# A transformer tower on one core: ScalarE makes the rounded high part of the normalised rows, GpSimd only the low part, and GpSimd's order of normalising changes

## The chip, the cores and the metric

The kernel runs on one core of one Trainium2 chip. The metric is the device time of one execution in microseconds (us). Engines are named as in the profile: PE is TensorE, ACT is ScalarE, DVE is VectorE, POOL is GpSimd, SP is SyncE, which only issues transfers here. Each engine works through its own instructions strictly in order and waits on semaphores for the others.

## The reference

32 sequences of 512 tokens with 64 features pass through an embedding and four layers. Each layer normalises its input row by row (no learned scale) and adds its result back to it:

```
h = tok(x)                                # token row plus position row
h = h + attn0(layernorm(h))               # softmax(q k^T / 8) x,  q = x Wq^T, k = x Wk^T
h = h + ffn0(layernorm(h))                # relu(Wi x), two layers routed to one of 16 experts, Wo
h = h + attn1(layernorm(h))               # the same with biases, values and an output projection
h = h + ffn1(layernorm(h))                # 8 experts of 64 -> 128 -> 64 with gelu, top 2 kept
```

The layer norm is `(x - mean) / sqrt(var + 1e-5)` over the 64 features.

## The kernel before, in words

All rows stay in SBUF in `H` (128 partitions, 32 sequences, 4 tiles of 128 tokens, 64 features). The kernel is written out engine by engine. After the embedding come four stages, called a0, f0, a1 and f1 (attention 0, routed layer, attention 1, mixture). In each, every engine runs a body once for each of the 32 sequences; a body i does the main work of sequence i and looks ahead. All that crosses engines is a count on a semaphore.

**The norm of a sequence** runs two to five sequences ahead of the stage that uses it:

- DVE sums the rows (`norm_sum`, L645).
- POOL centres them (`norm_centre`): a mean of 128x4 (L363), then `XC` = row minus mean (L369).
- DVE squares `XC`, sums and makes the variance (`norm_squares`: L649, L651, L653) and raises `var_ready`.
- POOL scales (`norm_scale`): a power of -0.5 on 128x4 (L375), `XN` = `XC` times it in full fp32 (L382), the same product once more into the rounded type fp32r, the high part in the left half of `XS` (L387), and the low part, `XN` minus the high part, in the right half (L390), which raises `xs_ready`.
- PE transposes `XS` (`turn`, L928), ACT copies the result into `X2` (`evac_x`, L463), and the stage's matmuls use it.

`XC`, `XS` and `X2` have two buffers, `XN` has four, since the attention reads it as its values. So in the attention stages the write of `XN` for sequence i+3 waits for the count `o_ps` that PE raises with the last matmul of `values` for sequence i-1 (L1013).

**Where the bodies stand.** POOL's body i does `norm_centre` of i+4 and then `norm_scale` of i+3. DVE's attention body i begins with `norm_squares` of i+4 and goes on with `norm_sum` of i+5, the low part of the queries (L729), `finish` of i-1 (L742, L744, L746) and the four row maxima of i+1 (L735). PE's attention body computes `spread_max` (L992), `project` of i+1 (L968, L969), the turn of i+2, the scores (L1004, L1005) with `turn_back` (L953) between them, and then, in this order, two `scores_for_max` of i+1 (L979), half of `values` of i, two more `scores_for_max`, which need the first two maxima, and the other half of `values`. ACT's attention body takes out the values (L485), the maxima (L504) and the queries (L491), makes the four exponentials (L511) and ends with `evac_x` of i+2.

In f0, PE's body i starts with the turn of i+2 (L928) and ends with the first routed layer of sequence i (L1087, the second four of eight matmuls). ACT's body takes out `X2` (L463) and the input layer (L521), then the values of an earlier sequence (L483), and ends with the two relus of L534, which wait for exactly that routed layer.

Of the kernel before, what the change touches and what calls it, by code (L numbers as in the profile page):

```python
# [22 lines left out]
ALU = mybir.AluOpType  # L23
ACT = mybir.ActivationFunctionType
# [3 lines left out]
NSEQ, SEQ, D = 32, 512, 64  # L28
# [13 lines left out]
CONSTS = 7  # L42
# [100 lines left out]
def sweep(eng, body, start=0, first=4, last=NSEQ - 6):  # L143


    for i in range(start, first):
        body(i, i % 2)
    with eng.Fori(first // 2, last // 2) as pair:
        body(pair * 2, 0)
        body(pair * 2 + 1, 1)  # L150
    for i in range(last, NSEQ):
        body(i, i % 2)
# [14 lines left out]
def known(i):  # L167
    return isinstance(i, int)


def has(i):

    return not known(i) or i < NSEQ


def tower_kernel(nc, tokens, route, pack, experts, out, ids_dram, pos_dram):
# [3 lines left out]
    with ExitStack() as ctx:  # L180
# [165 lines left out]
        @block.gpsimd  # L346
        def _(pool):
            pl = nc.gpsimd

            pl.memset(half[:, :], -0.5).then_inc(consts_set, 1)  # L350
            pl.memset(ninv[:, :], -1.0 / D).then_inc(consts_set, 1)
            pl.memset(MK[:, :, :], 0.0).then_inc(consts_set, 1)
            pl.memset(XN[:, :, :, 0:1], 1.0).then_inc(consts_set, 1)
            pl.memset(f32(XS[:, :, :, 0:1]), 1.0).then_inc(consts_set, 1)
            pl.memset(f32(XS[:, :, :, D:D + 1]), 0.0).then_inc(consts_set, 1)
            pl.memset(R1[:, :], 0.0).then_inc(consts_set, 1)

            pool.wait_ge(consts_set, CONSTS)

            def norm_centre(s, before, phase, i, par):  # L360

                pool.wait_ge(s.sum_ready, i + 1)
                pl.tensor_tensor(stat[:, par, 1, :], stat[:, par, 0, :], ninv[:, :], ALU.mult).then_inc(mean_done, 1)  # L363
                pool.wait_ge(mean_done, phase * NSEQ + i + 1)
                if not known(i) or i >= 2:
                    pool.wait_ge(s.var_ready, i - 1)
                elif before is not None:
                    pool.wait_ge(before.var_ready, NSEQ - 1 + i)
                pl.tensor_tensor(XC[:, par, :, :], hb(i), over(stat[:, par, 1, :], D), ALU.add)\  # L369
                    .then_inc(s.xc_ready, 1)  # L370

            def norm_scale(s, before, phase, i, par, lane):

                pool.wait_ge(s.var_ready, i + 1)
                pl.tensor_tensor(stat[:, par, 3, :], stat[:, par, 2, :], half[:, :], ALU.pow).then_inc(sigma_done, 1)  # L375
                pool.wait_ge(sigma_done, phase * NSEQ + i + 1)
                if (s is a0 or s is a1) and (not known(i) or i >= 4):
                    pool.wait_ge(s.o_ps, i - 3)
                elif (before is a0 or before is a1) and known(i) and i < 4:
                    pool.wait_ge(before.o_ps, NSEQ - 3 + i)  # L380
                scale = over(stat[:, par, 3, :], D - 1)
                pl.tensor_tensor(XN[:, lane, :, 1:D], XC[:, par, :, 1:D], scale, ALU.mult).then_inc(xn_done, 1)  # L382
                if not known(i) or i >= 2:
                    pool.wait_ge(s.xt_ready, i - 1)
                elif before is not None:
                    pool.wait_ge(before.xt_ready, NSEQ - 1 + i)
                pl.tensor_tensor(XS[:, par, :, 1:D], XC[:, par, :, 1:D], scale, ALU.mult).then_inc(s.xh_done, 1)  # L387
                pool.wait_ge(xn_done, phase * NSEQ + i + 1)
                pool.wait_ge(s.xh_done, i + 1)
                pl.tensor_tensor(XS[:, par, :, D + 1:2 * D], XN[:, lane, :, 1:D], f32(XS[:, par, :, 1:D]),  # L390
                                 ALU.subtract).then_inc(s.xs_ready, 1)

            def centre_on(s, before, after, phase, i, par):

                if has(i):
                    norm_centre(s, before, phase, i, par)
                elif after is not None:
                    norm_centre(after, s, phase + 1, i - NSEQ, par)

            def scale_on(s, before, after, phase, i, par, lane):  # L400
                if has(i):
                    norm_scale(s, before, phase, i, par, lane)
                elif after is not None:
                    norm_scale(after, s, phase + 1, i - NSEQ, par, lane)

            def norms(s, before, after, phase):
                def body(i, par, lane):
                    centre_on(s, before, after, phase, i + 4, par)
                    scale_on(s, before, after, phase, i + 3, 1 - par, (lane + 3) % 4)

                sweep4(pool, body)


            norm_centre(a0, None, 0, 0, 0)
            for i in range(3):
                norm_centre(a0, None, 0, i + 1, 1 - i % 2)
                norm_scale(a0, None, 0, i, i % 2, i)
            norms(a0, None, f0, 0)
            norms(f0, a0, a1, 1)
            norms(a1, f0, f1, 2)  # L420

            norms(f1, a1, None, 3)
# [3 lines left out]
        def _(act):  # L426
# [21 lines left out]
            for i in range(EARLY + HIGHS, EARLY + HIGHS + 2):  # L448
# [2 lines left out]
                           w("ident")[D:P, D:D + NEXP1].unsqueeze(2).to_broadcast([P - D, NEXP1, HID]),  # L451
                           ACT.Copy, scale=-OFF).then_inc(high_set, 1)
            sweep(act, embed, start=EARLY + HIGHS + 2, first=EARLY + HIGHS + 2)

            def evac_x(s, i, par):
                act.wait_ge(s.xt_ready, i + 1)
# [31 lines left out]
            def attention(s, before, after, layer, meanwhile):  # L488
                def evac_q(i, par):
                    act.wait_ge(s.q_ps, i + 1)  # L490
                    sc_.activation(QH[:, par, :], bank[1][:, :], ACT.Copy).then_inc(s.qh_ready, 1)  # L491

                if before is None:
                    evac_x(s, 0, 0)
                evac_q(0, 0)
                if before is None:
                    evac_x(s, 1, 1)

                def body(i, par):
                    if not known(i) or i >= 1:  # L500
                        evac_o(s, before, bank[6], i - 1, 1 - par)
                    act.wait_ge(s.m_ps, i + 1)
                    act.wait_ge(s.ql_ready, i + 1)
                    sc_.activation(Q2[0:1, par, :], bank[7][0:1, :], ACT.Copy).then_inc(s.m_ready, 1)  # L504
                    if has(i + 1):
                        evac_q(i + 1, 1 - par)
                    for kt in range(NT):
                        act.wait_ge(s.st_ps, i * NT + (kt + 1))
                        if kt == 0 and (not known(i) or i >= 2):
                            act.wait_ge(s.o_ps, i - 1)  # L510
                        sc_.activation(PT[:, par, kt, :], bank[4 + kt % 2][:, :], ACT.Exp,  # L511
                                       scale=SCALE).then_inc(s.e_ready, 1)
                    evac_x_on(s, after, i + 2, par)

                sweep(act, body)
                meanwhile()
                evac_o(s, before, bank[6], NSEQ - 1, 1)

# [3 lines left out]

            attention(a0, None, f0, 0, lambda: ffn0_in(0, 0))

            def ffn0(i, par):
                evac_x_on(f0, a1, i + 2, par)
                if has(i + 1):
                    ffn0_in(i + 1, 1 - par)
                if not known(i) or i >= 2:
                    evac_o(f0, a0, bank[4], i - 2, par)  # L530
                act.wait_ge(f0.l0_ps, i + 1)
                act.wait_ge(f0.wc_ready, i + 1)
                for g in range(NG):
                    ins = sc_.activation(group(F1[:, par, :], g), group(bank[2][:, :], g), ACT.Relu,  # L534
                                         bias=WC[:, par, g, HID:HID + 1])
                ins.then_inc(f0.h1_ready, 1)

            def group(ap, g):

                return ap.rearrange("k (t g p) -> k g t p", t=NT, g=NG)[:, g, :, :]  # L540

            sweep(act, ffn0)
            evac_o(f0, a0, bank[4], NSEQ - 2, 0)
            evac_o(f0, a0, bank[4], NSEQ - 1, 1)
            attention(a1, f0, f1, 1, lambda: None)
# [13 lines left out]
                    act.wait_ge(f1.down_ps, i * NEXP1 + (e - 7))  # L559
                sc_.activation(G[:, e, :], bank[3 + e % 2][:, :], ACT.Gelu).then_inc(f1.gelu_ready, 1)  # L560

            def ffn1(i, par):
                for e in range(4):
                    gelu(i, e)
                if not known(i) or i >= 1:
                    evac_o(f1, a1, bank[6 - par], i - 1, 1 - par)
                gelu(i, 4)
                gelu(i, 5)
                if has(i + 1):
                    masks(i + 1, 1 - par)  # L570
                gelu(i, 6)
                gelu(i, 7)
                if has(i + 2):
                    evac_x(f1, i + 2, par)

            sweep(act, ffn1)
            evac_o(f1, a1, bank[6], NSEQ - 1, 1)


# [725 lines left out]
```

## Time and profile before

| what | value |
|---|---|
| median of 3 runs | 1053.97 us (1051.72 to 1054.2) |
| the profiled execution: its own time | 1054.74 us |
| its span, first to last instruction | 1052.9 us |
| busy: PE, DVE, ACT, POOL | 956.7, 660.6, 547.1, 491.1 us |
| mean granted clock of TensorE | 0.98 |
| embedding and start | about 0 to 84 us |
| a0 / f0 / a1 / f1 | to about 319 / 461 / 706 / 1053 us |

The first column of a timeline row is the start, the second the duration. The stage limits are read off the first and last starts of each stage's matmuls, to a few microseconds.

### The profile page before, as it was taken

The page shows a single profiled execution, that of the slowest core. Times are in us where ns is not written, and L with a number is a line of the kernel's source. Part 1 is how long each engine was busy: PE and PEld are TensorE (multiplying, and loading weights), DVE is VectorE, ACT ScalarE, POOL GpSimd, SP SyncE. Part 2 cuts the span into 40 slices and gives each one's busy share as a digit, 9 for nine tenths or more (in the row PEclk, how much of TensorE's full clock was granted, in tenths as well). Part 3 has the DMA queues.
Part 4 walks back from the last instruction along what each step waited for, and adds up shares of the span by engine and source line. Part 5 has one row for each costly group of instructions (what it writes and reads, how often), then busy time and mean ns, then how long its engine had stood idle before and what let it go on. Part 6 is the DMA issues. An engine that isn't in the chain of part 4 may idle for free.

```text
span 1052.9 us, 20503 instructions
## 1 busy us (share of the span) xinstructions
PE 956.7 (91%) x5964; PEld 612.7 (58%) x5964; DVE 660.6 (63%) x1864; ACT 547.1 (52%) x1065; POOL 491.1 (47%) x779
## 2 busy tenths in 40 slices
PE   0479999999998888879999999999999999999998
PEld 0456666666665555556666666665555555555554
DVE  1586888887887888877888878873333434343311
ACT  0234555555555555535555555565555555555554
POOL 0026454554547888974545455453333333333310
PEclk9868999999999999999999999999999999999999
DMA  8930000000001212200000000000000000000000
GB/s 8 254 108 1 2 0 0 0 0 0 1 1 49 58 55 60 61 21 2 1 0 0 0 0 1 1 1 7 16 11 15 10 12 13 10 15 10 16 11 21
DMA packets 31309, 22.35 MB, mean 21 GB/s; under 512 B 14498, under 2 KB 26914, under 8 KB 31266
## 3 DMA queue, kind: packets, MB, share of 16 engines
q1 hardware_dynamic: 31266, 21.81, 9.5%
q8 instruction: 23, 0.38, 0.2%
q14 instruction: 20, 0.16, 0.1%
HBM read 17.54 MB, written 4.26 MB: 21 GB/s over the span
## 4 chain that ended last, share of the span: by engine, by line
PE 70%; DVE 10%; POOL 7%; issue 5%; DMA 4%; ACT 2%; DVEq 0%; SPq 0%; POOLq 0%
PE bank L1178 12%; PE bank L1158 7%; PE bank L1004 6%; PE bank L1013 6%; DVE nmax L735 6%; PE bank L1005 6%; PE bank L979 5%; PE bank L1159 5%; PE bank L928 5%; PE bank L992 4%; PE bank L953 3%; POOL stat L375 2%; DMA pos<-posn 2%; PE bank L1135 2%; PE bank L1168 2%
## 5 line engine op out<-in xcount | busy, mean ns | idle before, releaser
L560 ACT ACTIVATE PT<-bank 128x512 f32<-128x512 f32 x256 | 142.2, 595 | 99.9 <-PE bank L1159 99.1
L735 DVE TENSOR_REDUCE nmax<-bank 128x1 fp32r<-128x512 f32 x256 | 164.9, 686 | 34.0 <-PE bank L979 29.5
L382 POOL TENSOR_TENSOR XN<-XC,stat 128x252 f32<-128x252 f32 x128 | 85.3, 667 | 214.0 <-PE bank L1013 209.0
L511 ACT ACTIVATE PT<-bank 128x512 f32<-128x512 f32 x256 | 139.1, 595 | 46.1 <-PE bank L1005 46.1
L375 POOL TENSOR_TENSOR stat<-stat,half 128x4 f32<-128x4 f32 x128 | 134.3, 1049 | 38.0 <-DVE stat L653 35.4
L795 DVE TENSOR_TENSOR H<-H,bank 128x256 f32 (+1 forms) x64 | 26.9, 421 | 186.8 <-PE bank L958 186.8
L1013 PE MATMUL bank<-PT,XN 128*64 128x256 f32 x1024 | 138.3, 392 | 0.0
L1178 PE MATMUL bank<-PT,W 128*64 128x256 f32 x1024 | 137.2, 388 | 0.0
L387 POOL TENSOR_TENSOR XS<-XC,stat 128x252 fp32r<-128x252 f32 x128 | 77.3, 604 | 103.6 <-PE bank L928 103.6
L1158 PE MATMUL bank<-X,WH 128*128 128x512 f32 x256 | 116.0, 453 | 1.0 <-ACT K L551 0.8
L1004 PE MATMUL bank<-QH,X 128*128 128x512 f32 x256 | 115.8, 452 | 0.6 <-ACT Q L504 0.4
L485 ACT ACTIVATE OT<-bank 128x256 f32<-128x256 f32 x96 | 37.1, 386 | 133.8 <-PE bank L1013 132.0
L390 POOL TENSOR_TENSOR XS<-XN,XS 128x252 fp32r<-128x252 f32 x128 | 94.5, 738 | 18.7 <-POOL XS L387 0.5
L463 ACT ACTIVATE X<-bank 128x512 fp32r<-128x512 f32 x128 | 76.5, 597 | 51.2 <-PE bank L928 51.2
L1005 PE MATMUL bank<-Q,X 128*128 128x512 f32 x256 | 101.6, 397 | 0.0
L1159 PE MATMUL bank<-K,WL 80*128 80x512 f32 x256 | 100.8, 394 | 0.0
L928 PE MATMUL bank<-W,XS 128*128 128x128 f32 x512 | 80.3, 280 | 21.8 <-POOL XS L390 21.1
L1178 PEld LDWEIGHTS bank<-PT,W 128*64 128x64 f32 x1024 | 64.8, 136 | 57.9 <-issue 34.6
L1013 PEld LDWEIGHTS bank<-PT,XN 128*64 128x64 f32 x1024 | 62.2, 136 | 58.1 <-ACT PT L511 22.7
L979 PE MATMUL bank<-X,QH 128*128 128x512 f32 x256 | 88.3, 426 | 1.7 <-DVE nmax L735 1.4
L369 POOL TENSOR_TENSOR XC<-H,stat 128x256 f32<-128x256 f32 x128 | 79.1, 618 | 20.0 <-POOL stat L363 16.3
L363 POOL TENSOR_TENSOR stat<-stat,ninv 128x4 f32<-128x4 f32 x128 | 30.7, 240 | 122.7 <-DVE stat L645 122.7
(124 smaller groups left out, 1620.1 us busy)
## 6 DMA issues: line engine op xcount, KB each, us to landing
WR<-experts SPq DMA_DIRECT2D x64, 129.0 KB, 2.1
PT<-ids SPq DMA_DIRECT2D x16, 256.0 KB, 5.3
out<-H SPq DMA_DIRECT2D x32, 128.0 KB, 1.7
posb<-pos SPq DMA_DIRECT2D x16, 192.0 KB, 5.7
W<-pack SPq DMA_DIRECT2D x5, 263.0 KB, 6.4
W<-pack SPq DMA_DIRECT2D x1, 262.5 KB, 9.7
W<-pack SPq DMA_DIRECT2D x1, 65.0 KB, 4.7
tk<-tokens SPq DMA_DIRECT2D x1, 64.0 KB, 4.5
```

The source lines that it names most:

```text
L375: pl.tensor_tensor(stat[:, par, 3, :], stat[:, par, 2, :], half[:, :], ALU.pow).then_inc(sigma_done, 1)
L511: sc_.activation(PT[:, par, kt, :], bank[4 + kt % 2][:, :], ACT.Exp, scale=SCALE).then_inc(s.e_ready, 1)
L560: sc_.activation(G[:, e, :], bank[3 + e % 2][:, :], ACT.Gelu).then_inc(f1.gelu_ready, 1)
L735: v.tensor_reduce(nmax[:, par, t:t + 1], bank[2 + t % 2][:, :], axis=AX, op=ALU.max, negate=True).then_inc(s.max_ready, 1)
L928: last = nc.tensor.transpose(bank[0][:, t * P:(t + 1) * P], f32(XS[:, par, t, :]), w("ident"))
L979: mm(bank[2 + t % 2][:, :], QH[:, par, t * P:(t + 1) * P], X2[:, par, :], start=True, stop=True).then_inc(s.s_ps, 1)
L1004: mm(o, X2[:, par, cols], QH[:, par, :], start=True, stop=False)
L1005: mm(o, X2[:, par, cols], Q2[:, par, :], start=False, stop=True).then_inc(s.st_ps, 1)
L1013: last = mm(bank[6][h * D:(h + 1) * D, 0:HALF], XN[:, lane, kt, :], PT[:, par, kt, h * HALF:(h + 1) * HALF], start=(kt == 0), stop=(kt == ...
L1158: mm(o, WH[:, a:a + HID], X2[:, par, :], start=True, stop=False)
L1159: mm(o, WL[0:D + 2 * NEXP1, a:a + HID], K2[0:D + 2 * NEXP1, par, :], start=False, stop=True)\
L1178: last = mm(bank[5 + par][h * D:(h + 1) * D, 0:HALF], w2[:, e, :], G[:, e, h * HALF:(h + 1) * HALF], start=False, stop=(e == NEXP1 - 1))
```

## The change

Three things change. ScalarE copies `XN` into the high part (`high`, an activation with the function Copy), where GpSimd multiplied a second time; GpSimd keeps only the subtraction (`norm_low`). GpSimd's body i is now power and `XN` of i+3, then centring of i+4, then the low part of i+3. The copy of sequence i+3 is the last instruction in each of ScalarE's bodies i, and at the start ScalarE makes the copies of sequences 0, 1 and 2 before its first `evac_x`. The programs of PE and DVE are the same instructions in the same order.

```diff
--- before.py
+++ after.py
@@ -380,12 +380,9 @@
                     pool.wait_ge(before.o_ps, NSEQ - 3 + i)
                 scale = over(stat[:, par, 3, :], D - 1)
                 pl.tensor_tensor(XN[:, lane, :, 1:D], XC[:, par, :, 1:D], scale, ALU.mult).then_inc(xn_done, 1)
-                if not known(i) or i >= 2:
-                    pool.wait_ge(s.xt_ready, i - 1)
-                elif before is not None:
-                    pool.wait_ge(before.xt_ready, NSEQ - 1 + i)
-                pl.tensor_tensor(XS[:, par, :, 1:D], XC[:, par, :, 1:D], scale, ALU.mult).then_inc(s.xh_done, 1)
-                pool.wait_ge(xn_done, phase * NSEQ + i + 1)
+
+            def norm_low(s, i, par, lane):
+
                 pool.wait_ge(s.xh_done, i + 1)
                 pl.tensor_tensor(XS[:, par, :, D + 1:2 * D], XN[:, lane, :, 1:D], f32(XS[:, par, :, 1:D]),
                                  ALU.subtract).then_inc(s.xs_ready, 1)
@@ -403,10 +400,17 @@
                 elif after is not None:
                     norm_scale(after, s, phase + 1, i - NSEQ, par, lane)
 
+            def low_on(s, after, i, par, lane):
+                if has(i):
+                    norm_low(s, i, par, lane)
+                elif after is not None:
+                    norm_low(after, i - NSEQ, par, lane)
+
             def norms(s, before, after, phase):
                 def body(i, par, lane):
+                    scale_on(s, before, after, phase, i + 3, 1 - par, (lane + 3) % 4)
                     centre_on(s, before, after, phase, i + 4, par)
-                    scale_on(s, before, after, phase, i + 3, 1 - par, (lane + 3) % 4)
+                    low_on(s, after, i + 3, 1 - par, (lane + 3) % 4)
 
                 sweep4(pool, body)
 
@@ -415,6 +419,7 @@
             for i in range(3):
                 norm_centre(a0, None, 0, i + 1, 1 - i % 2)
                 norm_scale(a0, None, 0, i, i % 2, i)
+                norm_low(a0, i, i % 2, i)
             norms(a0, None, f0, 0)
             norms(f0, a0, a1, 1)
             norms(a1, f0, f1, 2)
```

The same for ScalarE:

```diff
@@ -451,6 +456,26 @@
                            w("ident")[D:P, D:D + NEXP1].unsqueeze(2).to_broadcast([P - D, NEXP1, HID]),
                            ACT.Copy, scale=-OFF).then_inc(high_set, 1)
             sweep(act, embed, start=EARLY + HIGHS + 2, first=EARLY + HIGHS + 2)
+
+            def high(s, before, phase, i, par, lane):
+
+                act.wait_ge(xn_done, phase * NSEQ + i + 1)
+                if not known(i) or i >= 2:
+                    act.wait_ge(s.xt_ready, i - 1)
+                elif before is not None:
+                    act.wait_ge(before.xt_ready, NSEQ - 1 + i)
+                act.wait_ge(consts_set, CONSTS)
+                sc_.activation(XS[:, par, :, 1:D], XN[:, lane, :, 1:D], ACT.Copy).then_inc(s.xh_done, 1)
+
+            def high_on(s, before, after, phase, i, par, lane):
+
+                if has(i):
+                    high(s, before, phase, i, par, lane)
+                elif after is not None:
+                    high(after, s, phase + 1, i - NSEQ, par, lane)
+
+            for i in range(3):
+                high(a0, None, 0, i, i % 2, i)
 
             def evac_x(s, i, par):
                 act.wait_ge(s.xt_ready, i + 1)
@@ -496,7 +521,7 @@
                 if before is None:
                     evac_x(s, 1, 1)
 
-                def body(i, par):
+                def body(i, par, lane):
                     if not known(i) or i >= 1:
                         evac_o(s, before, bank[6], i - 1, 1 - par)
                     act.wait_ge(s.m_ps, i + 1)
@@ -511,8 +536,9 @@
                         sc_.activation(PT[:, par, kt, :], bank[4 + kt % 2][:, :], ACT.Exp,
                                        scale=SCALE).then_inc(s.e_ready, 1)
                     evac_x_on(s, after, i + 2, par)
-
-                sweep(act, body)
+                    high_on(s, before, after, layer * 2, i + 3, 1 - par, (lane + 3) % 4)
+
+                sweep4(act, body)
                 meanwhile()
                 evac_o(s, before, bank[6], NSEQ - 1, 1)
 
@@ -522,7 +548,7 @@
 
             attention(a0, None, f0, 0, lambda: ffn0_in(0, 0))
 
-            def ffn0(i, par):
+            def ffn0(i, par, lane):
                 evac_x_on(f0, a1, i + 2, par)
                 if has(i + 1):
                     ffn0_in(i + 1, 1 - par)
@@ -534,12 +560,13 @@
                     ins = sc_.activation(group(F1[:, par, :], g), group(bank[2][:, :], g), ACT.Relu,
                                          bias=WC[:, par, g, HID:HID + 1])
                 ins.then_inc(f0.h1_ready, 1)
+                high_on(f0, a0, a1, 1, i + 3, 1 - par, (lane + 3) % 4)
 
             def group(ap, g):
 
                 return ap.rearrange("k (t g p) -> k g t p", t=NT, g=NG)[:, g, :, :]
 
-            sweep(act, ffn0)
+            sweep4(act, ffn0)
             evac_o(f0, a0, bank[4], NSEQ - 2, 0)
             evac_o(f0, a0, bank[4], NSEQ - 1, 1)
             attention(a1, f0, f1, 1, lambda: None)
@@ -559,7 +586,7 @@
                     act.wait_ge(f1.down_ps, i * NEXP1 + (e - 7))
                 sc_.activation(G[:, e, :], bank[3 + e % 2][:, :], ACT.Gelu).then_inc(f1.gelu_ready, 1)
 
-            def ffn1(i, par):
+            def ffn1(i, par, lane):
                 for e in range(4):
                     gelu(i, e)
                 if not known(i) or i >= 1:
@@ -572,8 +599,9 @@
                 gelu(i, 7)
                 if has(i + 2):
                     evac_x(f1, i + 2, par)
-
-            sweep(act, ffn1)
+                high_on(f1, a1, None, 3, i + 3, 1 - par, (lane + 3) % 4)
+
+            sweep4(act, ffn1)
             evac_o(f1, a1, bank[6], NSEQ - 1, 1)
```

**GpSimd in an attention stage.** The rows are one body of the program of before, with the first row of the next; L382 is the product that makes `XN`.

```order
L363 TENSOR_TENSOR stat<-stat,ninv 128x4 [waits a0_sum_ready]
L369 TENSOR_TENSOR XC<-H,stat 128x256 [waits a0_var_ready,mean_done]
L375 TENSOR_TENSOR stat<-stat,half 128x4 [waits a0_var_ready]
L382 TENSOR_TENSOR XN<-XC,stat 128x4x63 [waits a0_o_ps,sigma_done]
L387 TENSOR_TENSOR XS<-XC,stat 128x4x63 [waits a0_xt_ready]
L390 TENSOR_TENSOR XS<-XN,XS 128x4x63 [waits a0_xh_done,xn_done]
L363 TENSOR_TENSOR stat<-stat,ninv 128x4 [waits a0_sum_ready]
```

And of the changed program, where the subtraction has line 387:

```order
L375 TENSOR_TENSOR stat<-stat,half 128x4 [waits a0_var_ready]
L382 TENSOR_TENSOR XN<-XC,stat 128x4x63 [waits a0_o_ps,sigma_done]
L363 TENSOR_TENSOR stat<-stat,ninv 128x4 [waits a0_sum_ready]
L369 TENSOR_TENSOR XC<-H,stat 128x256 [waits a0_var_ready,mean_done]
L387 TENSOR_TENSOR XS<-XN,XS 128x4x63 [waits a0_xh_done]
L375 TENSOR_TENSOR stat<-stat,half 128x4 [waits a0_var_ready]
```

The centring (L363, L369) stood ahead of the instruction that waits for `o_ps` and now stands behind it.

**ScalarE in f0.** One body of before, and the first row of the next:

```order
L463 ACTIVATE X<-bank 128x512 [waits f0_xt_ready]
L521 ACTIVATE F<-bank 128x512 [waits f0_wi_ps]
L483 ACTIVATE OT<-bank,W 128x256 [waits f0_back_ps,f0_o_ps]
L534 ACTIVATE F<-bank,WC 128x4x64 [waits f0_wc_ready,f0_l0_ps]
L534 ACTIVATE F<-bank,WC 128x4x64
L463 ACTIVATE X<-bank 128x512 [waits f0_xt_ready]
```

The same place in the changed program:

```order
L488 ACTIVATE X<-bank 128x512 [waits f0_xt_ready]
L547 ACTIVATE F<-bank 128x512 [waits f0_wi_ps]
L508 ACTIVATE OT<-bank,W 128x256 [waits f0_back_ps,f0_o_ps]
L560 ACTIVATE F<-bank,WC 128x4x64 [waits f0_wc_ready,f0_l0_ps]
L560 ACTIVATE F<-bank,WC 128x4x64
L462 REGISTER_ALU
L468 ACTIVATE XS<-XN 128x4x63 [waits consts_set,f0_xt_ready,xn_done]
```

The copy stands behind the relus, which wait for `l0_ps`, the count of the routed layer with which PE ends its body.

**ScalarE at the start**, in the changed program; H is the end of the embedding, X the first `evac_x`:

```order
L436 ACTIVATE H<-bank 128x256 [waits emb_ready] x6
L468 ACTIVATE XS<-XN 128x4x63 [waits consts_set,xn_done] x2
L468 ACTIVATE XS<-XN 128x4x63 [waits consts_set,a0_xt_ready,xn_done]
L488 ACTIVATE X<-bank 128x512 [waits a0_xt_ready]
L516 ACTIVATE QH<-bank 128x512 [waits a0_q_ps]
```

Before, X followed H directly; the three copies of L468 now stand between them.

## Rows read from the trace of the kernel before

**Rows 1.** Windows of a0 and f0: us; busy PE, PEld, DVE, ACT, POOL; clock.

```profile
113.00:282.00 169.00, 165.43 (x968) 110.30 (x968) 136.79 (x277) 95.75 (x185) 87.30 (x139) 1.00 0.00 0
...
319.00:461.00 142.00, 120.38 (x640) 79.79 (x640) 118.86 (x282) 75.87 (x159) 124.69 (x188) 1.00 0.21 56
```

**Rows 2.** The chain that ended last, in f0: start us, us, what.

```profile
338.22 1.13 POOL stat L375
...
410.54 1.13 POOL stat L375
```

**Rows 3.** Timeline of f0: start us, us, then idle time before in brackets.

```profile
390.41 0.72 POOL L390 TENSOR_TENSOR XS<-XN,XS 128x252 fp32r<-128x252 f32 x1
...
391.18 0.66 PE L928 MATMUL bank<-W,XS 128*128 128x128 f32 x4 [0.66 <-POOL XS L390]
...
393.10 1.89 PE L1087 MATMUL bank<-F,WC 128*128 128x256 f32 x8
...
395.03 0.84 ACT L534 ACTIVATE F<-bank,WC 128x256 f32<-128x256 f32 x2 [1.54 <-PE bank L1087]
```

**Rows 4.** Timeline of a0, one body.

```profile
197.52 0.41 DVE L649 TENSOR_TENSOR SQ<-XC 128x256 f32<-128x256 f32 x1
...
197.68 0.72 POOL L382 TENSOR_TENSOR XN<-XC,stat 128x252 f32<-128x252 f32 x1 [3.26 <-PE bank L1013]
...
198.91 0.41 DVE L645 TENSOR_REDUCE stat<-H 128x4 f32 x1
...
200.27 0.61 POOL L369 TENSOR_TENSOR XC<-H,stat 128x256 f32<-128x256 f32 x1 [0.27 <-POOL stat L363]
...
200.68 0.18 DVE L742 RECIPROCAL rec<-bank 128x4 f32<-128x4 f32 x1 [0.49 <-PE bank L953]
...
201.92 1.29 DVE L735 TENSOR_REDUCE nmax<-bank 128x1 fp32r<-128x512 f32 x2
...
202.18 0.60 ACT L463 ACTIVATE X<-bank 128x512 fp32r<-128x512 f32 x1
...
203.70 1.08 PE L1013 MATMUL bank<-PT,XN 128*64 128x256 f32 x8
...
204.94 0.73 POOL L382 TENSOR_TENSOR XN<-XC,stat 128x252 f32<-128x252 f32 x1 [3.08 <-PE bank L1013]
```

**Rows 5.** Timeline of the start of a0.

```profile
77.95 0.38 ACT L431 ACTIVATE H<-bank 128x256 f32<-128x256 f32 x1 [2.62 <-PE bank L904]
...
78.61 0.61 POOL L382 TENSOR_TENSOR XN<-XC,stat 128x252 f32<-128x252 f32 x1
...
79.17 0.60 POOL L387 TENSOR_TENSOR XS<-XC,stat 128x252 fp32r<-128x252 f32 x1
...
79.71 0.60 ACT L463 ACTIVATE X<-bank 128x512 fp32r<-128x512 f32 x1 [1.38 <-PE bank L928]
...
79.92 0.72 POOL L390 TENSOR_TENSOR XS<-XN,XS 128x252 fp32r<-128x252 f32 x1
...
80.60 0.20 POOL L363 TENSOR_TENSOR stat<-stat,ninv 128x4 f32<-128x4 f32 x1
...
80.88 0.61 POOL L369 TENSOR_TENSOR XC<-H,stat 128x256 f32<-128x256 f32 x1
...
81.45 1.02 POOL L375 TENSOR_TENSOR stat<-stat,half 128x4 f32<-128x4 f32 x1
...
81.53 0.42 DVE L649 TENSOR_TENSOR SQ<-XC 128x256 f32<-128x256 f32 x1 [2.54 <-POOL XC L369]
...
82.52 0.69 DVE L729 TENSOR_TENSOR Q<-bank,QH 128x512 fp32r<-128x512 f32 x1
...
82.55 0.61 POOL L382 TENSOR_TENSOR XN<-XC,stat 128x252 f32<-128x252 f32 x1
```

**Rows 6.** Groups by form, f0 from 360 to 396: busy us, mean ns.

```profile
L649 DVE TENSOR_TENSOR SQ<-XC 128x256 f32<-128x256 f32 x8 | 6.0, 755 | 0.0
```

**Rows 7.** Timeline of f1.

```profile
783.36 0.60 ACT L560 ACTIVATE PT<-bank 128x512 f32<-128x512 f32 x1 [0.80 <-PE bank L1159]
```

## The prediction
> **What bounds the kernel now.** I read the page first: PE is busy for 91% of the span, POOL for 47%, so a relief of POOL can pay only where POOL is what PE waits for. The windows view shows where that is [rows 1]: in a0 PE is busy for 165.4 of 169 us and POOL for 87.3; in f0 it is the other way round, 120.4 of 142 us against POOL's 124.7. The chain that ended last then says what sets f0's pace: it goes through POOL's power (L375) again and again, and from 338.22 to 410.54 us lie 16 bodies, so a body of f0 takes 72.32 / 16 = 4.52 us [rows 2]. The timeline shows the wait itself: PE sat idle for 0.66 us until POOL's low part (L390), 390.41 + 0.72 = 391.13, let it turn at 391.18 [rows 3]. PE's own body runs from there to the end of the last routed matmul, 393.10 + 1.89 = 394.99, that is 3.81 us. In the attention the pace is 204.94 - 197.68 = 7.26 us a body in the piece shown [rows 4], and two things are to be seen there. POOL's product `XN` starts only 0.16 us after PE's last `values` matmul (203.70 + 1.08 = 204.78), after 3.08 us of idle time. And DVE has no long wait: squares, sum, low part of the queries, reciprocal at 200.68, then maxima at 201.92, on the third of which PE's next scores depend.
>
> **The change in f0: a new loop through three engines.** One multiplication of about 0.60 us (the form of 79.17 in [rows 5]) leaves POOL's body. But the copy that replaces it stands at the end of ScalarE's body, behind the relus, and these wait for the end of PE's body. POOL's low part waits for the copy, and PE's next body begins with the turn that waits for the low part. So all of it comes after one another, once per body:
>
> - turn to relus: 391.18 to 395.03, 3.85 us [rows 3]
> - the two relus: 0.84 us [rows 3]
> - the copy of 128x252: no copy of this form is in the trace. ScalarE's 128x256 copy out of PSUM took 0.38 us, the 128x512 one 0.60 us [rows 5]; these are the bounds, and I take 0.40, by the nearer form
> - from ScalarE to POOL: no row; POOL follows PE by 0.16 us [rows 4], DVE follows POOL by 0.04 us (81.53 after 80.88 + 0.61, [rows 5]). I take 0.08
> - the low part 0.72 us, and 0.05 us to PE's turn [rows 3]
>
> The sum is 5.94 us a body instead of 4.52. Sequence i+3 of ScalarE's body i is what PE's body i+1 turns, so every one of the 31 steps from a body of f0 to the next has it: 31 x 1.42 = 44 us more. Bounds: with 0.38 and 0.04 it is 5.88 us (42 us), with 0.60 and 0.16 it is 6.22 us (53 us). The relief of POOL is worth nothing there, since POOL then waits for the copy.
>
> **The change in the attention stages: the centring comes behind the wait.** POOL's centring of i+4 was done before POOL waited for the values of i-1; DVE's squares at the head of its body found it finished (200.27 + 0.61 = 200.88, squares at 204.79 or so). Now POOL does it behind `XN`, which can't start before those values are done. DVE's squares wait for it, and behind them on DVE stand the sum, the low part of the queries, `finish` and the maxima; PE's third and fourth `scores_for_max` wait for the first two maxima, and the second half of the values stands behind these on PE. That closes a loop from `XN` to the next `XN`:
>
> - `XN` to the mean 0.56 (78.61 to 79.17, the spacing of two such products), mean to `XC` 0.28, `XC` 0.61, to the squares 0.04 us [rows 5]
> - squares to the next instruction of DVE 0.99 us (81.53 to 82.52), the sum 0.41 [rows 4], the low part of the queries 0.69 us [rows 5]
> - reciprocal to maxima 1.24, two maxima 1.29, from their end (203.21) to the second half of the values 0.49, these 1.08, to `XN` 0.16 us [rows 4]
>
> Sum: 7.84 us, against 7.26 in the same piece. I take 0.60 us a body. This loop exists in bodies 1 to 30 of each attention, 60 times: 36 us. Its upper bound takes the slower durations of the same instructions, where POOL and DVE worked at once: 0.72 for `XN`, 0.47 from mean to `XC`, 1.39 from squares to sum [rows 4], which makes 8.59 us, and 80 us in all. The lower bound is 0.3 us a body, 18 us, if DVE's instructions overlap a little more than these spacings.
>
> A rule bears on the choice between 0.99 and 1.39. In f0, the squares took 0.755 us in the mean [rows 6], with POOL at work, and 0.41 us in a0 [rows 4]. The Trainium skill, SBUF — State Buffer, section "Who interferes with whom", says that a VectorE instruction with two SBUF inputs and a GpSimd instruction that reads SBUF lock each other out, while a reduction never contends. By that rule the squares of the new loop run alone, for POOL has nothing to do then but wait for the copy; by it the sum stays at 7.84 us, by the contended rows at 8.59.
>
> **What else of it is hidden in the attention.** The copy itself: ScalarE's `evac_x` ends at 202.18 + 0.60 = 202.78, the next thing it waits for comes at 204.8 [rows 4]; there is room for 0.40 us. Behind it POOL has the low part and the power: 202.78 + 0.40 + 0.08 + 0.68 (79.92 to 80.60) + 1.10 (81.45 to 82.55) = 205.04 us [rows 4, 5], and in the longer body `XN` can start at 197.68 + 7.84 = 205.52. That cover is only 0.5 us; if it is gone, each us beyond it costs 60 us.
>
> **f1.** ScalarE has 0.80 us of idle time between its first and second gelu [rows 7], after the place where the copy comes in, so its 0.40 us cost nothing; POOL's whole body has over 10 us there. Nothing is late next: the turn of that sequence comes a full body later. I count 0.
>
> **The start.** ScalarE's first `evac_x` was at 79.71 us [rows 5]. Now it comes behind three copies, and the third needs `XN` of sequence 2, for which POOL must first have finished two low parts, each behind a copy. Step by step from the end of the embedding at 77.95 + 0.38 = 78.33: copy to 78.73; low part (0.08 + 0.68) 79.49; centring of 2 (0.28 + 0.57) 80.34; power 1.10 and `XN` 0.61, 82.05; copy 0.48, 82.53; low part 83.29; centring of 3, 84.14; power and `XN` 85.85; copy 86.33. The first `evac_x` is 6.6 us late, and PE's first projection stands behind it, so all of the rest. Bounds 5 and 9 us.
>
> **The sum** is made against the profiled execution's own 1054.74 us (span 1052.9), 0.8 us over the median of the runs: 1054.7 + 6.6 + 44 + 36 + 0 = 1141 us. I forecast 1141 us, 8% slower.
>
> **The rivals.**
>
> - *Only f0 and the start cost* (chance 0.08): DVE makes up for the late squares. For it: DVE waits 0.49 us for PE before the reciprocal [rows 4], which is slack. Against: that slack is used up in the sum above. 1054.7 + 6.6 + 44 = 1105 us.
> - *The attention loop is contended or the 0.5 us of cover is gone* (0.12): 8.59 us a body, 1054.7 + 6.6 + 44 + 80 = 1185 us. For it: POOL and DVE do slow each other in [rows 6]. Against: POOL is idle while this loop is on DVE.
> - *The relief of POOL decides* (0.03), the other side: if the copy came to POOL in time in f0, POOL's body would be 0.60 us shorter, 3.92 us, just above PE's 3.81. 31 x 0.60 = 19 us off, 1036 us, provided that the attention hides its part too. It decides from the point at which the copy is done before POOL gets to the low part, which the place behind the relus excludes by about 3 us.
> - *The losses and the relief cancel, or nothing changes* (0.02): about 1054 us.
>
> The forecast, that all three parts cost about what is worked out, has 0.75.
>
> **How the numbers follow.** The likeliest case has its own range of 1120 to 1170 us (lower: 5 + 42 + 18; upper: 9 + 53 + 53, that is nearly 0.9 us an attention body). The range for 8 in 10 reaches towards both slower rivals, 1108 to 1180 us. A measurement of this kernel tells about 0.3% from no change. Faster by more than that has only the relief, 0.03; within it 0.02; slower 0.95.
>
> **What would show it.** In the changed profile: in f0, PE's turn waits about 2.1 us a body for POOL's low part, POOL's low part for ScalarE's copy, and a body takes 5.9 us; ScalarE's copies of `XN` take 0.40 us, 128 of them. In the attention, DVE's squares wait for `XC` in each body, for roughly 2 us, and a body takes 7.8 us or a little more; the centring starts about 0.6 us after `XN`. The first `evac_x` is near 86 us. f1 is as long as before. The prediction is wrong if the copy in f0 is found done when POOL comes to the low part, or if DVE's squares do not wait in the attention.

## The result, and the profile after

The changed kernel takes 1151.99 us in the median of 4 runs (1148.59 to 1153.64), the kernel before 1054.09 us in its 4 runs beside it: a ratio of 1.0927, with a 95% interval of 1.0895 to 1.0959. The forecast was 1141 us.

The page of the changed kernel: span and busy times, then the granted clock in the 40 slices.

```profile
span 1150.1 us, 20414 instructions
...
PE 1001.0 (87%) x5964; PEld 628.2 (55%) x5964; DVE 627.8 (55%) x1864; ACT 587.4 (51%) x1193; POOL 406.2 (35%) x651
...
PEclk9768999999998888888999999999999999999999
```

PE has the same 5964 matmuls as before and 44 us more of busy time, POOL 85 us less. In slices 13 to 19, which are f0, the clock is at 8 tenths; before, it stood at 9 in f0. The windows view cuts out a0 and f0, beside [rows 1] (the same columns).

```profile
112.00:332.00 220.00, 213.16 (x1209) 137.56 (x1211) 155.08 (x347) 127.99 (x259) 88.78 (x145) 1.00 0.00 0
345.00:540.00 195.00, 134.00 (x571) 84.71 (x572) 106.70 (x251) 78.86 (x171) 97.13 (x145) 0.85 0.14 38
```

In f0 PE is busy for 134 of 195 us, and the granted clock is 0.85. To compare stages I take ScalarE's `evac_o` of sequence 0 in each attention, and the last, which every kernel has:

| stretch | before, us | after, us | more |
|---|---|---|---|
| to the first `evac_o` of a0 | 94.83 | 98.54 | 3.7 |
| a0, to its last | 226.2 | 235.2 | 9.0 |
| f0, to the first of a1 | 158.1 | 231.8 | 73.7 |
| a1, to its last | 226.1 | 234.4 | 8.4 |
| f1 and the end of the span | 347.7 | 350.1 | 2.4 |

The sum is the 97.2 us between the two spans. The first row also holds the embedding, whose end moves by some us from trace to trace: in f0_early, fill8, fill4 and fill2, which have the changed kernel's program up to there, the first `evac_o` starts at 97.92, 97.68, 99.84 and 101.23 us. Who waits is in the waits view of the changed kernel: us in total, times, longest.

```profile
POOL XS L387 <- ACT XS L468: 580.8, 128, 12.8
...
DVE SQ L677 <- POOL XC L369: 132.4, 70, 3.3
...
PE bank L956 <- POOL XS L387: 68.8, 32, 2.2
...
POOL XN L382 <- PE bank L1041: 37.1, 60, 1.0
```

POOL's low part waits for ScalarE's copy in all 128 bodies, PE's turn for the low part in the 32 of f0, and DVE's squares for the centring, 132 us in all; before, the turn waited 21 us in all, the first wait was not there, and the squares waited 3.2 us in all. They can be seen one by one. First a body of f0 in the timeline:

```profile
420.20 0.41 ACT L468 ACTIVATE XS<-XN 128x252 fp32r<-128x252 f32 x1
...
420.69 0.84 POOL L387 TENSOR_TENSOR XS<-XN,XS 128x252 fp32r<-128x252 f32 x1 [3.78 <-ACT XS L468]
...
421.59 0.66 PE L956 MATMUL bank<-W,XS 128*128 128x128 f32 x4 [2.15 <-POOL XS L387]
...
425.43 0.84 ACT L560 ACTIVATE F<-bank,WC 128x256 f32<-128x256 f32 x2 [1.54 <-PE bank L1115]
...
426.16 0.41 ACT L468 ACTIVATE XS<-XN 128x252 fp32r<-128x252 f32 x1
...
426.65 0.84 POOL L387 TENSOR_TENSOR XS<-XN,XS 128x252 fp32r<-128x252 f32 x1 [2.31 <-ACT XS L468]
...
427.54 0.79 PE L956 MATMUL bank<-W,XS 128*128 128x128 f32 x4 [2.15 <-POOL XS L387]
```

The turn at 421.59, the relus at 425.43, the copy at 426.16, the low part at 426.65 and the next turn at 427.54: 5.95 us, each behind the other, in place of the pace of [rows 2]. The turn follows at once where [rows 3] had it wait 0.66 us; here it waits 2.15. But the next body is longer. The windows view, cut at four turns in a row:

```profile
421.59:427.54 5.95, 3.80 (x20) 2.50 (x21) 3.83 (x10) 2.70 (x6) 3.38 (x6) 1.00 0.17 44
427.54:435.04 7.50, 5.35 (x20) 3.32 (x21) 3.84 (x10) 2.81 (x6) 3.38 (x6) 0.77 0.13 35
435.04:441.00 5.96, 3.82 (x21) 2.50 (x21) 3.84 (x10) 2.68 (x6) 3.38 (x6) 1.00 0.17 44
441.00:448.51 7.51, 5.36 (x21) 3.26 (x21) 3.84 (x10) 2.81 (x6) 3.39 (x6) 0.77 0.12 35
```

The same 20 or 21 matmuls take 3.80 us in one body and 5.35 in the next, at a clock of 0.77, a mixture of the levels 2.4 and 1.2 GHz; the 1.55 us are the whole difference between 5.95 and 7.50 us. Over 29 bodies, from the turn at 345.50 to that at 544.30 us, the mean is 6.86 us: 12 of them take 5.95 to 6.05 us and 17 take 7.36 to 7.52.

The attention, one body of a0 in the timeline, beside [rows 4]:

```profile
213.75 0.61 POOL L382 TENSOR_TENSOR XN<-XC,stat 128x252 f32<-128x252 f32 x1 [0.82 <-PE bank L1041]
...
214.77 0.61 POOL L369 TENSOR_TENSOR XC<-H,stat 128x256 f32<-128x256 f32 x1 [0.26 <-POOL stat L363]
...
215.42 0.43 DVE L677 TENSOR_TENSOR SQ<-XC 128x256 f32<-128x256 f32 x1 [2.19 <-POOL XC L369]
...
216.46 0.42 DVE L673 TENSOR_REDUCE stat<-H 128x4 f32 x1
...
217.39 0.17 DVE L770 RECIPROCAL rec<-bank 128x4 f32<-128x4 f32 x1
...
218.09 0.59 ACT L488 ACTIVATE X<-bank 128x512 fp32r<-128x512 f32 x1
...
218.51 2.57 DVE L763 TENSOR_REDUCE nmax<-bank 128x1 fp32r<-128x512 f32 x4
218.57 0.42 ACT L468 ACTIVATE XS<-XN 128x252 fp32r<-128x252 f32 x1
219.07 0.72 POOL L387 TENSOR_TENSOR XS<-XN,XS 128x252 fp32r<-128x252 f32 x1 [3.68 <-ACT XS L468]
...
220.27 1.08 PE L1041 MATMUL bank<-PT,XN 128*64 128x256 f32 x8
...
221.45 0.61 POOL L382 TENSOR_TENSOR XN<-XC,stat 128x252 f32<-128x252 f32 x1 [0.68 <-PE bank L1041]
```

The squares waited 2.19 us for the centring that ended at 214.77 + 0.61 = 215.38, and from `XN` to `XN` it is 7.70 us. The four maxima now follow one another without a gap, 2.57 us; before, they came in pairs with PE between them.

### The profile page after: what moved, and what is told of

Read it like the earlier page. It is cut to its first block, busy times and chain, and to the rows that moved or that the text cites. A ratio compares the mean times of both kernels' runs of the same rounds, so it can differ in the third digit from the quotient of the medians.

```text
span 1150.1 us, 20414 instructions
## 1 busy us (share of the span) xinstructions
PE 1001.0 (87%) x5964; PEld 628.2 (55%) x5964; DVE 627.8 (55%) x1864; ACT 587.4 (51%) x1193; POOL 406.2 (35%) x651
## 4 chain that ended last, share of the span: by engine, by line
PE 53%; DVE 17%; issue 10%; POOL 10%; ACT 5%; DMA 4%; DVEq 1%; POOLq 0%; SPq 0%; ACTq 0%
PE bank L1206 11%; PE bank L1186 6%; DVE nmax L763 6%; PE bank L1041 5%; PE bank L1187 5%; PE bank L1115 4%; PE bank L956 4%; POOL XC L369 3%; POOL XS L387 3%; DVE Q L757 3%; PE bank L1007 3%; ACT X L488 2%; PE bank L986 2%; DVE SQ L677 2%; PE bank L1124 2%
## 5 line engine op out<-in xcount | busy, mean ns | idle before, releaser
L956 PE MATMUL bank<-W,XS 128*128 128x128 f32 x512 | 84.4, 290 | 68.8 <-POOL XS L387 68.8
L375 POOL TENSOR_TENSOR stat<-stat,half 128x4 f32<-128x4 f32 x128 | 137.0, 1071 | 0.3 <-DVE stat L681 0.3
L677 DVE TENSOR_TENSOR SQ<-XC 128x256 f32<-128x256 f32 x128 | 54.0, 422 | 132.4 <-POOL XC L369 132.4
L1007 PE MATMUL bank<-X,QH 128*128 128x512 f32 x256 | 104.2, 451 | 14.3 <-DVE nmax L763 4.8
L956 PEld LDWEIGHTS bank<-W,XS 128*128 128x128 f32 x512 | 63.9, 147 | 90.4 <-POOL XS L387 56.1
L382 POOL TENSOR_TENSOR XN<-XC,stat 128x252 f32<-128x252 f32 x128 | 77.8, 608 | 42.5 <-PE bank L1041 37.1
L369 POOL TENSOR_TENSOR XC<-H,stat 128x256 f32<-128x256 f32 x128 | 78.9, 617 | 19.7 <-POOL stat L363 16.0
```

Source lines behind the costliest of these rows:

```text
L956: last = nc.tensor.transpose(bank[0][:, t * P:(t + 1) * P], f32(XS[:, par, t, :]), w("ident"))
L1007: mm(bank[2 + t % 2][:, :], QH[:, par, t * P:(t + 1) * P], X2[:, par, :], start=True, stop=True).then_inc(s.s_ps, 1)
```

## The experiments

Each is one edit, on the changed kernel unless it says otherwise.

**f0_early: the copy in f0 ahead of the relus.**

```diff
             def ffn0(i, par, lane):
...
+                high_on(f0, a0, a1, 1, i + 3, 1 - par, (lane + 3) % 4)
                 act.wait_ge(f0.l0_ps, i + 1)
...
-                high_on(f0, a0, a1, 1, i + 3, 1 - par, (lane + 3) % 4)
```

> The changed kernel, but in f0 ScalarE's copy stands ahead of the relus instead of behind them. Theory A (in f0 the copy behind the relus makes one loop turn - routed layer - relus - copy - low part - turn): the loop opens; the next limit is the variance, through power, product, centring and low part over two bodies, (4.9 + 3.6) / 2 = 4.3 us a body instead of the 6.85 us in the mean of the changed kernel, and with PE's idle time the lower clock in f0 goes too. 31 x 2.5 = 77 us less: about 1075 us. Rival B (the bodies of 7.5 us in f0 come from something else, such as the loads of experts): every second body stays long, and no more than 31 x 1.4 = 44 us go: about 1108 us.

Measured: 1080.96 us, a ratio of 1.0270 (1.0234 to 1.0306) to the kernel before, 71 us less than the changed kernel. A body of f0 takes 4.60 us (22 bodies between 346.65 and 447.97 us), and the windows view of this kernel gives f0 its clock back:

```profile
345.00:450.00 105.00, 87.51 (x460) 57.43 (x460) 88.49 (x207) 63.54 (x136) 75.80 (x115) 1.00 0.22 57
```

No body is long any more, so rival B is out. The body is 4.60 and not 4.3 us. As the timeline reads, and no run tests it, this is because the squares run beside POOL's low part and take 0.92 us there, which is then on the path that leads through the variance; POOL's power waits 1.01 us for it:

```profile
422.45 0.72 POOL L387 TENSOR_TENSOR XS<-XN,XS 128x252 fp32r<-128x252 f32 x1
...
422.53 0.92 DVE L677 TENSOR_TENSOR SQ<-XC 128x256 f32<-128x256 f32 x1
...
423.94 0.17 DVE L681 TENSOR_SCALAR stat<-var 128x4 f32<-128x4 f32 x1
...
424.18 1.27 POOL L375 TENSOR_TENSOR stat<-stat,half 128x4 f32<-128x4 f32 x1 [1.01 <-DVE stat L681]
```

**centre_first: GpSimd centres first again.**

```diff
                 def body(i, par, lane):
-                    scale_on(s, before, after, phase, i + 3, 1 - par, (lane + 3) % 4)
                     centre_on(s, before, after, phase, i + 4, par)
+                    scale_on(s, before, after, phase, i + 3, 1 - par, (lane + 3) % 4)
                     low_on(s, after, i + 3, 1 - par, (lane + 3) % 4)
```

> The changed kernel with one thing back: GpSimd centres before power and product, as before; the copy stays on ScalarE where it is. Theory A (the attention lost its time by the centring behind the wait for the values): both attentions go back to about 7.3 us a body, the squares hardly wait; f0 keeps its loop and its clock. About 35 us less than the changed kernel: 1117 us. Rival C (ScalarE's extra 0.4 us a body, or the low part that comes late behind it, costs the time): the attention stays at 7.8 us a body, no difference.

Measured: 1134.64 us, a ratio of 1.0766 (1.0740 to 1.0792), 17 us less than the changed kernel. Both attentions are back at 7.31 us a body (30 bodies between 101.75 and 320.89 us), and f0 is as bad as in the changed kernel, at a clock of 0.86. Rival C is out: ScalarE has its 0.41 us in every body here and it costs nothing. With the copy on ScalarE, the order costs 17 us in all, not 35, for the attention of the changed kernel took 7.63 us a body in the mean, not 7.9. The groups view from 120 to 300 us shows the squares without their wait:

```profile
L677 DVE TENSOR_TENSOR SQ<-XC 128x256 f32<-128x256 f32 x25 | 10.6, 423 | 1.1 <-POOL XC L369 1.1
```

**order_only: the kernel before, with GpSimd's order alone.**

```diff
                 def body(i, par, lane):
-                    centre_on(s, before, after, phase, i + 4, par)
                     scale_on(s, before, after, phase, i + 3, 1 - par, (lane + 3) % 4)
+                    centre_on(s, before, after, phase, i + 4, par)
+                    low_on(s, before, after, phase, i + 3, 1 - par, (lane + 3) % 4)
```

with `norm_low` holding GpSimd's second product and the subtraction.

> The kernel before with GpSimd's order alone changed: power and product, then centring, then high part (still GpSimd's multiplication) and low part. ScalarE as before. Theory A: the attention has the new loop without any copy, 7.8 us a body, 60 x 0.5 = 30 us more; f0 is limited by the variance through power, product, centring and both halves, (4.9 + 4.2) / 2 = 4.6 us a body, 3 us more: about 1088 us, and PE keeps its clock. Rival C: without the copy on ScalarE the attention stays at 7.3 us, about 1057 us.

Measured: 1109.41 us, a ratio of 1.0524 (1.0497 to 1.0551), so 55 us more than the kernel before without any copy on ScalarE. The attention takes 8.01 us a body (30 bodies, 94.15 to 334.57 us), 0.7 us more than before; f0 4.9 us at a clock of 1.00. 60 x 0.69 and 31 x 0.4 us make 54 us. In f0 0.1 us a body was expected; the squares run beside POOL there and take 0.85 us in the mean. Rival C is out here too. That it is slower in the attention than the changed kernel was not expected. Its squares, in the same view and stretch, and those of the changed kernel:

```profile
L660 DVE TENSOR_TENSOR SQ<-XC 128x256 f32<-128x256 f32 x23 | 18.7, 811 | 46.7 <-POOL XC L369 46.7
```

```profile
L677 DVE TENSOR_TENSOR SQ<-XC 128x256 f32<-128x256 f32 x24 | 10.2, 426 | 48.9 <-POOL XC L369 48.9
```

0.81 against 0.43 us, which is the whole 0.38 us between 8.01 and 7.63: here POOL has its second product to do just when the squares have become free to run, in the changed kernel it waits for the copy. Both wait about 2 us for the centring.

**fill8, fill4 and fill2: work that nobody reads.** PE gets 8, 4 or 2 matmuls more at the end of each body of f0.

```diff
                 routed(i, par, 0)
+                for _ in range(8):          # 4, 2
+                    mm(bank[5][:, 0:HALF], w("ident"), W[:, 0:HALF], start=True, stop=True)
```

> The changed kernel with extra work: in f0, PE ends each body with 8 matmuls of 128x256 whose result nobody reads, in a bank that f0 does not use. They take about 1.9 us of the 2.15 us that PE waits for the low part. Theory D (the bodies of 7.5 us are bodies at the lower granted clock, which came with PE's idle time): the granted clock in f0 stays at 1.00, all bodies take about 6.0 us, and the kernel gets faster by doing more, 31 x 0.9 = 27 us less: about 1125 us. Rival B (something else makes every second body long): no gain, or up to 31 us slower where the extra matmuls come on top.

Measured: 1160.59 us, a ratio of 1.1016 (1.0988 to 1.1044), 9 us slower than the changed kernel. The price of the matmuls was mis-sized: each stands as two in the profile, and the 8 take 3.62 us, not 1.9:

```profile
404.86 3.62 PE L1146 MATMUL bank<-W 128*128 128x256 f32 x16
...
408.31 0.60 PE L956 MATMUL bank<-W,XS 128*128 128x128 f32 x4
```

But no body is long or short any more (6.96 to 7.12 us), and the clock is 1.00. So the clock half of the theory held and the time was inconclusive; hence the two smaller ones.

> The changed kernel with 4 idle matmuls at the end of PE's body in f0. The 8 of the run before took 3.6 us a body, more than the 2.15 us of waiting, and f0 ran at 7.04 us a body at a granted clock of 1.00. Theory D (the long bodies of the changed kernel are bodies at the lower clock): 4 take 1.8 us and fit into the wait, every body takes 5.96 us, clock 1.00, 31 x 0.9 = 27 us less than the changed kernel: about 1124 us. Rival B (the wait for the low part is what it is, and the clock follows something else): no gain, 1152 us.

Measured: 1128.16 us, a ratio of 1.0674 (1.0648 to 1.0701).

> The same with 2 idle matmuls, 0.9 us of the 2.15 us. Theory D: part of the long bodies go, 5.96 to 6.85 us a body, 1124 to 1152 us. Rival B: 1152 us.

Measured: 1127.18 us, a ratio of 1.0667 (1.0640 to 1.0695). Both are 24 to 25 us faster than the changed kernel, by doing more, and in both a body of f0 takes 5.96 us in the mean, with none over 6.05. The stretch of f0 in the table above, 231.8 us in the changed kernel, is 206.8 us in fill4 and 205.6 in fill2. The windows view of fill2 in f0:

```profile
345.00:510.00 165.00, 128.70 (x664) 89.80 (x664) 105.23 (x248) 74.52 (x167) 94.30 (x140) 1.00 0.17 44
```

With theory D two matmuls were expected to give back a part and gave back all. Rival B is out: the loop through the low part still sets the 5.96 us, and the long bodies were the lower clock.

**start_only: another order at ScalarE's start.**

```diff
-            for i in range(3):
-                high(a0, None, 0, i, i % 2, i)
...
                 if before is None:
+                    high(s, None, 0, 0, 0, 0)
                     evac_x(s, 0, 0)
+                    high(s, None, 0, 1, 1, 1)
                 evac_q(0, 0)
                 if before is None:
                     evac_x(s, 1, 1)
+                    high(s, None, 0, 2, 0, 2)
```

> The changed kernel with ScalarE's first instructions in another order: copy 0, first evac_x, copy 1, first queries, second evac_x, copy 2. Theory A: the first evac_x comes 1.4 us after the embedding's end and the low part, not behind three copies, some 6.5 us earlier, and the rest moves with it: about 1146 us. Rival: the start was not on the path, since POOL is late with its own norms: 1152 us.

Measured: 1149.23 us, a ratio of 1.0880 (1.0850 to 1.0910), whose interval overlaps that of the changed kernel; the times alone do not tell it. The timelines do, counted from the end of the last embedding copy: the first `evac_x` comes after 7.85 us in the changed kernel (75.44 to 83.29) and after 2.50 us here (77.56 to 80.06); the first `evac_o` after 23.1 and 19.75 us. So 3.4 us of the start are gained, less than the 6.5; POOL's next norms, each behind a copy, look like the next thing late, which was not tested.

**all_four and three.** All repairs together: f0_early, centre_first and start_only, and in all_four also the attention's copy between `evac_q` and the exponentials instead of at the end of the body.

> Four repairs of the changed kernel together: copy ahead of the relus in f0, centring first, the start in the order of start_only, and in the attention the copy between the queries and the exponentials. Theory A: both attentions at 7.33 us a body as before; f0 limited by POOL, copy and PE at 4.1 to 4.4 us a body instead of 4.52, 5 to 12 us less than the kernel before: about 1046 us. Rival (the ScalarE copy costs as much as it relieves): within 3 us of the kernel before.

Measured: 1052.16 us, a ratio of 0.9958 (0.9940 to 0.9975).

> The four repairs together once more, to tell a small gain from none. Theory A: f0 at 4.29 us a body instead of 4.48, 31 x 0.2 = 6 us, less about 1 us of a longer start: 0.3 to 0.6% faster than the kernel before. Rival: no difference.

Measured again: 1052.14 us, a ratio of 0.9961 (0.9944 to 0.9978).

> As all_four, but in the attention the copy stays the last instruction of ScalarE's body. Theory A: the low part and with it the next centring come 1.3 us later, DVE's squares wait 0.1 to 0.2 us in the attention as in centre_first, and DVE's slack before the reciprocal (0.5 us) takes that up: 7.33 us a body, the same time as all_four within 0.3%, about 0.4% under the kernel before. Rival: the small wait goes into the maxima, 60 x 0.15 = 9 us more than all_four.

Measured: 1051.52 us, a ratio of 0.9954 (0.9937 to 0.9971).

These beat the kernel before, by 0.4%, and the place of the copy in the attention makes no difference. The 4.6 us of all_four lie just under the 5 to 12 of theory A and above the 3 of its rival. Where they come from is f0: 4.29 us a body (26 bodies between 338.30 and 449.74 us) against 4.49 before (26 between 334.39 and 451.12), and a stretch of f0 that is 4.8 us shorter than before (153.3 us). The windows view of all_four in f0, and one body's chain on the timeline:

```profile
345.00:450.00 105.00, 93.27 (x493) 61.28 (x494) 91.43 (x221) 68.82 (x148) 83.67 (x123) 1.00 0.24 62
```

```profile
400.29 0.72 POOL L387 TENSOR_TENSOR XS<-XN,XS 128x252 fp32r<-128x252 f32 x1 [0.52 <-ACT XS L468]
...
402.25 1.13 POOL L375 TENSOR_TENSOR stat<-stat,half 128x4 f32<-128x4 f32 x1
...
403.45 0.60 POOL L382 TENSOR_TENSOR XN<-XC,stat 128x252 f32<-128x252 f32 x1
...
404.09 0.41 ACT L468 ACTIVATE XS<-XN 128x252 fp32r<-128x252 f32 x1 [0.80 <-POOL XN L382]
404.58 0.72 POOL L387 TENSOR_TENSOR XS<-XN,XS 128x252 fp32r<-128x252 f32 x1 [0.52 <-ACT XS L468]
```

POOL's relief is real, but only 0.2 us of the 0.6 arrive: its low part now waits 0.52 us for the copy's way through ScalarE and back (403.45 + 0.60 to 404.58).

## Why the prediction was right, and where it was off

The mechanisms were right: all three losses came where the prediction put them, by the waits that it named. The total, 1141 against 1152 us, is closer than its terms, and that is luck: f0 cost 73.7 us where 44 were counted and 53 was the bound, the two attentions 17.4 where 36 were counted and 18 was the bound, and most of the two errors cancels.

- **The loop in f0**: right, and shown. The order of instructions is the one forecast, and a body at full clock takes 5.95 us where 5.94 was worked out. That it meets to 0.01 us is luck in part: the copy starts 0.73 us after the relus, not 0.84, and the low part takes 0.84 us, not 0.72. f0_early takes the loop away, and 71 us with it, the loss by the clock included.
- **The size of that term**: off. It was 44 us, measured 73.7 on the whole stretch of f0. The step that failed is the sum itself, 31 x 1.42, made with the durations of a trace in which PE hardly waited. PE now waits 2.15 us a body, and 17 of the 29 bodies are long, by about 1.5 us each, which makes some 26 us. fill4 and fill2 show it: PE's waits filled in part, all bodies take 5.96 us, and the stretch of f0 is 48.8 and 47.6 us over the kernel before, near the 44; the other 25 to 26 us are the clock.
- **The entry of f1**: counted as 0, and off. All of f1 with the end is 2.4 us longer, and the stretch from the last `evac_o` of a1 to the first of f1 alone 2.8 us. The windows view of that stretch, before and after:

```profile
705.21:721.45 16.24, 14.60 (x90) 8.81 (x92) 7.57 (x44) 9.84 (x17) 6.47 (x11) 1.00 0.01 1
800.02:819.09 19.07, 17.63 (x90) 10.29 (x92) 6.66 (x45) 10.48 (x18) 5.88 (x9) 0.82 0.00 1
```

The same 90 matmuls take 3.0 us more at a clock of 0.82. The other traces go with it: 16.20 us at a clock of 1.00 in centre_first and order_only, 17.77 to 17.80 us in f0_early, fill2, fill4 and fill8, at 0.90. So this loss comes and goes with the clock, and neither GpSimd's order alone nor the copy alone brings it; why the two together do was not tested.

- **The centring behind the wait**: right, and shown from both sides, centre_first and order_only. The squares wait 2.0 to 2.2 us, as said.
- **Its size**: 36 us, measured 17.4. Two parts of the sum failed. The base was one body of 7.26 us, where the mean of 30 was 7.33. And the sum of 7.84 us took durations and spacings of the trace before for DVE's instructions, where their starts now lie closer: sum to low part 0.34 instead of 0.41, low part to reciprocal 0.59 instead of 0.69, reciprocal to maxima 1.12 instead of 1.24; with 0.46 instead of 0.28 from mean to `XC` the other way, the body shown is 7.70 us. In the parts of the stage that are not a loop in the program, a body takes 7.43 us, which brings the mean down to 7.63; why was not tested.
- **The choice between contended and free squares**: right. They took 0.43 us in the changed kernel; in order_only, where POOL works beside them, 0.81. The Trainium skill, SBUF — State Buffer, section "Who interferes with whom", has a VectorE instruction with two SBUF inputs contend with a GpSimd instruction that reads SBUF; both rows agree.
- **The start**: the way there took what was worked out, 3.75 us from copy to copy (75.47 to 79.22) against 3.8, and the first `evac_o` comes 23.1 us after the embedding's end against 16.5 before, 6.6 us more. That only 3.7 us of it show is because the embedding ended 2.9 us earlier in this trace, at 75.44. Of these, 2.0 us were there before any instruction of the change ran (GpSimd's second mean at 71.82 us before, at 69.83 here). The other 0.9 is to be read on VectorE, though no run tests it: beside GpSimd's second product and low part, two of its instructions took 0.61 and 0.93 us before, and take 0.17 and 0.48 here, where GpSimd waits for the copy.

```profile
74.92 0.61 POOL L387 TENSOR_TENSOR XS<-XC,stat 128x252 fp32r<-128x252 f32 x1
74.94 0.61 DVE L653 TENSOR_SCALAR stat<-var 128x4 f32<-128x4 f32 x1
...
75.67 0.84 POOL L390 TENSOR_TENSOR XS<-XN,XS 128x252 fp32r<-128x252 f32 x1
75.87 0.93 DVE L640 TENSOR_SCALAR OP<-posb,W 96x512 bf16<-96x512 bf16 x1
```

- **Hidden parts**: the 0.41 us of the copy cost nothing in the attention (centre_first) and f1's bodies are 10.75 us as before.
- **The rivals**: that only f0 and the start cost is out, since centre_first gets 17 us back in the attention. That the attention loop is contended did not come about in the changed kernel; order_only shows it, at 8.01 us a body. That the relief decides did not come about either, but it is what all_four shows once the copy stands where it doesn't wait: 5 us, not 19.

## What to carry to other kernels

When a piece of work moves to another engine, its place in that engine's order can weigh more than its length: the copy of 0.4 us cost 71 us in f0 behind the wrong wait, and ahead of it helped to a gain of 5 us. When an instruction is put behind one that waits, follow what is queued behind it on every engine until the circle closes; that gave the body at full clock in f0. And where a change makes TensorE wait, ask in addition what its matmuls cost at the lower clock: here the sum from durations of a stage in which it hardly waited left out 26 us.

## What was not expected of the hardware

In f0 of the changed kernel, PE was busy for 3.8 of 5.95 us and the clock of the bodies alternated irregularly between 1.00 and 0.77; with two idle matmuls more, 0.9 us a body, it stayed at 1.00 and the kernel became 25 us faster. And a VectorE instruction that waits for GpSimd, and then runs beside GpSimd's next one, took 0.81 us where it takes 0.43 alone, so that moving GpSimd's second product away made the attention 0.4 us a body faster in an order of instructions that was worse otherwise (8.01 against 7.63 us).
